# A four-layer graph network on one core: the attention query as one wide product per slot, and the layer norm of x ahead of the slot search

## What is computed

```python
h = maximum(_layernorm(x), 0);  x = x + L0(h, weight, src, dst, edge_type_16)   # sum of h[src] @ weight[type] by dst
h = maximum(_layernorm(x), 0);  x = x + L1(h, edge_index, W_l, b_l, W_r)        # mean of h[src] by dst, elu
h = maximum(_layernorm(x), 0);  x = x + L2(h, edge_index, edge_attr_32, ...)    # edge MLP, sum by dst, node MLP, layer norm
h = maximum(_layernorm(x), 0);  x = x + L3(h, edge_index, edge_type_8, rule_ids, ...)  # attention
```

## Time and profile before

| | |
|---|---|
| median of 3 runs | 2432.45 us (2432.16 to 2432.92) |
| the profiled execution | 2440.53 us, span 2438.6 us |
| busy: PE, VectorE, ScalarE, GpSimd | 1427.3, 741.7, 191.1, 1610.6 us |
| instructions | 36361 |
| first gather of layers 0 to 3 | at 77, 625, 1192 and 1806 us |

### The profile page before, as it was taken

How to read it: one execution, slowest core, us unless ns; L and a number is a source line. 1 busy time by engine, 2 the same in 40 slices (tenths; PEclk the granted TensorE clock), 3 DMA queues, 4 the chain that set the end, 5 groups by cost and what they waited for, 6 DMA issues and landing times.

```text
span 2438.6 us, 36361 instructions
## 1 busy us (share of the span) xinstructions
PE 1427.3 (59%) x7642; PEld 1254.6 (51%) x7643; DVE 741.7 (30%) x2432; ACT 191.1 (8%) x311; POOL 1610.6 (66%) x1693
## 2 busy tenths in 40 slices
PE   5586666666433333333577657666574336767686
PEld 2386666666433333333466546555443236656575
DVE  5311111111511111111532222222442234444456
ACT  3000000000000000000211111111220000000000
POOL 2577777776577777776377777777127777777530
PEclk9655555555555555555655565565655555555555
DMA  6621111111111111111233333332063323222210
GB/s 195 219 43 27 26 26 26 26 26 23 32 26 26 26 26 26 26 26 24 49 72 68 66 65 65 65 65 54 6 256 83 78 75 78 79 77 77 57 42 14
DMA packets 159011, 144.41 MB, mean 59 GB/s; under 512 B 109905, under 2 KB 111855, under 8 KB 158802
## 3 DMA queue, kind: packets, MB, share of 16 engines
q0 software_dynamic: 53888, 69.64, 13.9%
q1 hardware_dynamic: 105058, 73.94, 10.4%
HBM read 113.55 MB, written 37.28 MB: 62 GB/s over the span
## 4 chain that ended last, share of the span: by engine, by line
POOL 54%; issue 22%; PE 16%; DVE 5%; DMA 2%; ACT 1%; SPq 0%; DVEq 0%; POOLq 0%; ACTq 0%
POOL flat L467 49%; PE ps L1200 8%; POOL uvT L467 5%; PE ps L1190 5%; PE ps L1042 1%; DMA table<-flat 1%; PE ps L1016 1%; PE ps L1025 1%; DVE var L545 0%; PE ps L1055 0%; DVE uvT L538 0%; DMA flat<-table,flat 0%; DVE mean L536 0%; DVE ps L870 0%; DVE h L560 0%
## 5 line engine op out<-in xcount | busy, mean ns | idle before, releaser
L467 POOL DMA_INDIRECT flat<-table,flat x1248 | 1194.3, 957 | 491.0 <-issue 379.7
L1055 PE MATMUL ps<-flat,oh 128*128 128x64 f32 x1664 | 469.2, 431 | 490.7 <-DMA flat<-table,flat 482.4
L1055 PEld LDWEIGHTS ps<-flat,oh 128*128 128x128 f32 x1664 | 406.5, 331 | 503.9 <-issue 503.9
L627 DVE TENSOR_SCALAR oh<-iota_n,drel 128x128 f32<-128x128 f32 x1248 | 264.0, 299 | 1052.2 <-PE ps L1055 631.9
L467 POOL DMA_INDIRECT uvT<-table,idx x416 | 399.5, 960 | 230.3 <-issue 125.6
L1190 PE MATMUL ps<-qn,oh_bytes 128*128 x1248 | 164.8, 235 | 188.6 <-issue 111.0
L1190 PEld LDWEIGHTS ps<-qn,oh_bytes 128*128 128x128 bf16 x1248 | 128.7, 104 | 227.0 <-issue 198.6
L1057 PEld LDWEIGHTS ps<-ones,oh 128*128 128x128 f32 x832 | 227.3, 333 | 0.0
L1057 PE MATMUL ps<-ones,oh 128*128 128x1 f32 x832 | 221.3, 335 | 0.0
L1200 PE MATMUL ps<-flat,oh 128*128 128x65 f32 (+1 forms) x832 | 188.1, 420 | 9.9 <-DVE oh L814 5.2
L1200 PEld LDWEIGHTS ps<-flat,oh 128*128 128x128 f32 x832 | 180.6, 331 | 15.5 <-issue 13.7
(11 more groups left out here) (259 smaller groups left out, 873.6 us busy)
## 6 DMA issues: line engine op xcount, KB each, us to landing
table<-flat SPq DMA_DIRECT2D x52, 512.0 KB, 3.6
oh_bytes<-slot_node SPq DMA_DIRECT2D x104, 256.0 KB, 3.4
flat<-table,flat POOLq DMA_INDIRECT x1248
flat<-edge_attr_padded SPq DMA_DIRECT2D x416, 16.0 KB
uvT<-table,idx POOLq DMA_INDIRECT x416
edge_attr_padded<-edge_attr SPq DMA_DIRECT2D x1, 6250.0 KB
xs<-x SPq DMA_DIRECT2D x1, 768.0 KB
flat<-L_gnn_weight SPq DMA_DIRECT2D x2, 256.0 KB, 3.9
```

The source lines that it names most:

```text
L467: nc.gpsimd.indirect_dma_start(dest[:, b, j, :], None, table, at_).then_inc(gat[b], 16)
L627: last = V.tensor_scalar(oh[:, b, j, :], iota_n[:], drel[:, bass.ds(g * SG + j, 1)], None, ALU.is_equal)
L1055: last = T.matmul(acc[:, bass.ds(n[j] * D, D)], oh[:, b, j, :], rows_[:, j, :], start=False, stop=True, skip_group_check=True)
```

## The change

Two edits are made together.

**Layer 3.** The three parts of the query of one slot are no longer accumulated by three products. One product of 204 columns (`qn[:, :, n, :]`, 3 x 68) leaves them side by side in PSUM: 8 products and 8 weight loads per group. `qr_ps` has two buffers, one for each half of a group, in place of four. VectorE adds the three parts: the rule part by a reduction over 3 (48 inputs per half, in place of a copy of 16), the query by multiplying all 192 columns by the key (768 elements per half and partition, in place of 256) and summing 192 in place of 64 (1536 inputs per group, in place of 512). TensorE signals each half by itself, and starts the next group's half when VectorE has multiplied this one's. `LATE` goes: in chunk 3 the last four steps weigh two groups each, as in chunk 2, and `mix(3)` weighs none.

**Setup.** SyncE loads all of `x` ahead of `dst`. VectorE takes the first half of the layer norm, then the four instructions up to `reach`, then the second half and `rectified`, and only then the slot search. VectorE copies the first halves of blocks 0 to 5 (`EARLY`) too, right behind the slot search, and again from block 18 (`AHEAD`, was 14). The transposes of line 1006 move behind block 5, those of line 1077 from behind block 11 to behind block 15.

```diff
-        qr_ps = [ps[:, 2048 + 512 * k:2048 + 512 * k + 4 * (D + NR)] for k in range(4)]
-        room = [ps[:, 2048 + 512 * k + 4 * (D + NR):2048 + 512 * (k + 1)] for k in range(4)]
+        QP = 256
+        qr_ps = [ps[:, 2048 + 4 * QP * q:2048 + 4 * QP * (q + 1)].rearrange("p (s c) -> p s c", s=4)[:, :, 0:3 * (D + NR)]
+                 .rearrange("p s (a d) -> p s a d", a=3) for q in range(2)]
+        room = [ps[:, 2048 + 512 * k:2048 + 512 * (k + 1)] for k in range(4)]
...
-        AHEAD = 14
+        EARLY, AHEAD = 6, 18
...
-            if c == 2:
-                return [PIECES[0] + lg] if left > RING else [PIECES[0] + 8 + 2 * (lg - 8) + k for k in range(2)]
-            return [FIRST[2] + lg]
-
-        LATE = [FIRST[2] + PIECES[3] + k for k in range(PIECES[2] - PIECES[3])]
+            once = PIECES[c] - RING
+            return [FIRST[c - 1] + lg] if lg < once else [FIRST[c - 1] + once + 2 * (lg - once) + k for k in range(2)]
...
+            sp.wait_ge(s("xs_clear"), 1)
+            sp.dma_start(xs[0:NLAST, TN - 1, :], a["x"][(TN - 1) * P:N, :]).then_inc(s("x_in"), 16)
 ...
             sp.wait_ge(s("init"), INIT)
...
+            def table_half(n):
+                dve.wait_ge(s("tab_ps"), n + 1)
+                stage_free(dve, 0, n)
+                V.tensor_copy(stage[:, n % 4, 0:512], acc[:, (n % 2) * 1024:(n % 2) * 1024 + 512]).then_inc(s("tabA"), 1)
...
             dve.wait_ge(s("x_in"), 32)
-            for t0, t1 in HALVES:
-                centred(xs, t0, t1)
+            centred(xs, *HALVES[0])
+            dve.wait_ge(s("dst_in"), 32)
+            dve.wait_ge(s("const"), 9)
...
+            centred(xs, *HALVES[1])
             rectified()
...
+            for n in range(EARLY):
+                table_half(n)
+            dve.wait_ge(s("rows_ps"), 1)
+            link(V.tensor_copy(n_slots, n_ps))
...
+            dve.wait_ge(s("tabA"), AHEAD)
             for n in range(AHEAD, NT):
+                table_half(n)
...
             def before3(g, b):
-                dve.wait_ge(s("qr_ps"), g + 1)
+                dve.wait_ge(s("qr_ps"), 2 * g + 2)
                 onehots_T(1, g, b)
 
             def score(g, lg, b):
-                dve.wait_ge(s("qr_ps"), g + 3)
                 landed(dve, 3, g, b)
+                dve.wait_ge(s("scored"), g + 2)
                 for q in range(2):
-                    qr = qr_ps[2 * (b % 2) + q].rearrange("p (s d) -> p s d", s=4)
-                    V.tensor_copy(rule_e[:, bass.ds(lg * SG + 4 * q, 4), :], qr[:, :, D:D + NR])
-                    V.tensor_tensor(msg[:, b % 2, 4 * q:4 * q + 4, :], qr[:, :, 0:D], got3[:, b, 4 * q:4 * q + 4, D:2 * D], ALU.mult).then_inc(s("prod"), 1)
-                dve.wait_ge(s("prod"), 2 * (g + 1))
-                V.tensor_reduce(base[:, bass.ds(g * SG, SG)], msg[:, b % 2], AX, ALU.add).then_inc(s("scored"), 1)
+                    four = slice(4 * q, 4 * q + 4)
+                    dve.wait_ge(s("qr_ps"), 2 * g + q + 5)
+                    V.tensor_reduce(rule_e[:, bass.ds(lg * SG + 4 * q, 4), :], qr_ps[q][:, :, :, D:D + NR].rearrange("p s a r -> p s r a"), AX, ALU.add)
+                    V.tensor_tensor(msg3[:, four], qr_ps[q][:, :, :, 0:D], got3[:, b, four, D:2 * D].unsqueeze(2).broadcast_to([P, 4, 3, D]), ALU.mult).then_inc(s("prod"), 1)
+                dve.wait_ge(s("prod"), 2 * g + 4)
+                V.tensor_reduce(base[:, bass.ds(g * SG, SG)], msg3.rearrange("p s a d -> p s (a d)"), AX, ALU.add).then_inc(s("scored"), 1)
...
             for n in range(NT):
                 act.wait_ge(s("tab_ps"), n + 1)
...
-                if n < AHEAD:
+                if n == EARLY:
+                    act.wait_ge(s("tabA"), EARLY)
+                if EARLY <= n < AHEAD:
                     A.copy(stage[:, n % 4, 0:512], acc[:, at_:at_ + 512]).then_inc(s("tabA"), 1)
...
             def query(g, b, n):
-                pe.wait_ge(s("scored"), g + 1)
                 pe.wait_ge(s("ohT"), G + g + 3)
                 for q in range(2):
+                    pe.wait_ge(s("prod"), 2 * g + q + 2)
                     for j in range(4):
-                        dest = qr_ps[2 * (b % 2) + q][:, j * (D + NR):(j + 1) * (D + NR)]
-                        for part in range(3):
-                            last = T.matmul(dest, ohT[:, b % 2, 4 * q + j, :], qn[:, part, bass.ds(n[4 * q + j], 1), :].rearrange("p t d -> p (t d)"),
-                                            start=(part == 0), stop=(part == 2))
-                last.then_inc(s("qr_ps"), 1)
+                        last = T.matmul(qr_ps[q][:, j], ohT[:, b % 2, 4 * q + j, :], qn[:, :, bass.ds(n[4 * q + j], 1), :].rearrange("p a t d -> p a (t d)"), start=True, stop=True)
+                    last.then_inc(s("qr_ps"), 1)
```

More of the change, by code:

```diff
@@ L508, in _, with stage_free @@
             V.memset(dst_rows[:, SC - 1, :], 0).then_inc(s("init"), 1)
[L509 removed]
             V.memset(dprev[:, SC - 1, :], 0).then_inc(s("init"), 1)
             V.memset(dnext[:, SC - 1, :], 0).then_inc(s("init"), 1)
[L513 to L519, removed]
[L520 to L531 removed]
+            def stage_free(eng, l, n):
+                before = l * len(range(n % 4, NT, 4)) + n // 4
+                if before:
+                    eng.wait_ge(tab[n % 4], 16 * before)
+            def table_half(n):
+                dve.wait_ge(s("tab_ps"), n + 1)
+                stage_free(dve, 0, n)
+                V.tensor_copy(stage[:, n % 4, 0:512], acc[:, (n % 2) * 1024:(n % 2) * 1024 + 512]).then_inc(s("tabA"), 1)
             sums, squares = [0], [0]
@@ L562, in _ @@
             dve.wait_ge(s("x_in"), 32)
-            for t0, t1 in HALVES:
-                centred(xs, t0, t1)
-            rectified()
+            centred(xs, *HALVES[0])
+            dve.wait_ge(s("dst_in"), 32)
+            dve.wait_ge(s("const"), 9)
+            link(V.tensor_scalar(reach_i[:], dst_rows[:, :, P - 1], 7, None, ALU.arith_shift_right))
+            link(V.tensor_tensor(reach[:], reach_i[:], iota_tile[:], ALU.add))
+            link(V.tensor_scalar(slot_t[:], iota_tile[:], float(TE - 1), 1e6, ALU.is_ge, ALU.mult))
+            V.tensor_tensor(reach[:], reach[:], slot_t[:], ALU.add).then_inc(s("reach"), 1)
+            centred(xs, *HALVES[1])
+            rectified()
+            link(V.memset(pack[:, SC - 1, :, :], 0))
+            dve.sem_inc(s("pack_clear"), 1)
+            dve.wait_ge(s("reach_row"), 1)
+            for c in range(SC):
+                link(V.tensor_scalar(work[0][:, :, :].rearrange("p c k -> p (c k)"), aux[:, 1024:1024 + SC * P], iota_slot[:, c:c + 1], None, ALU.is_lt, ALU.add, accum_out=slot_t[:, c:c + 1]))
+            link(V.tensor_copy(slot_ti[:], slot_t[:]))
+            link(V.tensor_tensor(slot_n[:], iota_slot[:], slot_t[:], ALU.subtract))
+            V.tensor_scalar(slot_n128[:], slot_n[:], float(P), None, ALU.mult).then_inc(s("slot_t"), 1)
+            for n in range(EARLY):
+                table_half(n)
+            dve.wait_ge(s("rows_ps"), 1)
+            n_ps = aux[0:1, 512:512 + SLOTS].rearrange("o (g j) -> o g j", j=SG)
+            link(V.tensor_copy(n_slots, n_ps))
             link(V.tensor_copy(n_words, n_slots[:, :, 0]))
@@ L1001, in _ @@
             for c in range(SC):
-                last = T.matmul(aux[:, c * P:(c + 1) * P], reach[:, c:c + 1].broadcast_to([P, P]), ident[:], start=True, stop=True)
+                last = T.matmul(aux[:, 1024 + c * P:1024 + (c + 1) * P], reach[:, c:c + 1].broadcast_to([P, P]), ident[:], start=True, stop=True)
             last.then_inc(s("reach_row"), 1)
-            pe.wait_ge(s("slot_t"), 1)
-            for c in range(SC):
-                last = T.transpose(aux[0:1, 512 + START[c]:512 + START[c] + P], slot_n[:, c:c + 1], ident[:])
-            last.then_inc(s("rows_ps"), 1)
             def node_transposes(src, *ready):
@@ L1071, in _ @@
             pe.wait_ge(s("w0_in"), 32)
-            for n in range(AHEAD - 2):
+            for n in range(EARLY):
+                table_ps(0, n)
+            pe.wait_ge(s("slot_t"), 1)
+            for c in range(SC):
+                last = T.transpose(aux[0:1, 512 + START[c]:512 + START[c] + P], slot_n[:, c:c + 1], ident[:])
+            last.then_inc(s("rows_ps"), 1)
+            for n in range(EARLY, AHEAD - 2):
                 table_ps(0, n)
```

53 lines of the change are left out of this document (10 added, 43 removed).

## The result

The changed kernel takes 2424.55 us (median of 7 runs, 2423.04 to 2425.29) and the kernel before 2432.45 (7 runs, 2431.11 to 2433.05): ratio 0.9965, 95% interval 0.9956 to 0.9975. It is 7.9 us faster; 43.4 us were forecast, and the range of 2381 to 2408 did not hold the time. The profiled execution took 2425.13 us with a span of 2423.3.

A forecast was written before the change was run, and what follows sets the result against it. GpSimd's gathers were taken to pace layers 0 to 2 and TensorE to bind from 2132 us in layer 3; 35.4 us there plus 8.0 in the setup, 43.4 off the median 2432.45, gave 2389, range 2381 to 2408.

The forecast's parts named there:

- the third item on the query: Layer 3: TensorE waits for the previous group's half product, done 2.1 us after a query starts; nothing lost.
- the item above it: Layer 3, VectorE: a score takes about 3.9 us where it took 1.65; covered, just, by TensorE's step.
- Query of 1.4 us, step 2.0 less: Layer 3, TensorE: 8 products for 24 take 1.4 us; a step shortens by 2.0, bounds 1.0 and 2.1.
- VectorE's score 3.9 us: Layer 3: a score with three query parts takes about 3.9 us, +2.2 on 1.65.
- rival 1: Layer 3: VectorE or the array takes over, steps shorten by about 1.2; 2403 or 2407 us, chance 0.21.
- Chunk 3 even, mix(3) 8.8 us won: Layer 3's end: faster queries offset the moved sums, 0.1 us won; last mix takes 13.1 for 21.9 us.
- GpSimd's stall: Layer 3, near the end of chunk 2: GpSimd's 15.56 us wait for a score would disappear.
- Setup, 8.0 us: Before layer 0: layer norm 9.1 us earlier, first table block at 19.9 for 28.24; 8 us left.
- the margin of 1.7 us: Setup: index copies end at 52.9, VectorE's block 18 comes at 54.6; 1.7 us free for a slower fetch.
- Rival 2: Gathers: longer VectorE instructions hold GpSimd, 2 us on each of 52 groups; 2493 us, chance 0.04.
- Rival 3: Layer 3's query: columns decide, so it costs the same; 2429 us, chance 0.04.

The follow-up runs named there:

- experiments 1 and 6: 1: changed kernel with the second half's extra wait relaxed, 2389.82 us; 6: the same with query and score of the first bf16 part only, 2390.62 us.
- experiment 3: Changed kernel with the old order of chunk 2's sums, 2416.56 us; reverse, kernel before with only the new order, 2442.65 us.
- experiment 4: Changed kernel with the second half's extra wait relaxed and the old order of chunk 2's sums, 2398.04 us.

## Why the prediction was wrong

**The step that failed** is the third item on the query: "TensorE now waits for the half product of the group before; that is done 2.1 us after a query starts, while the sums take longer. Nothing is lost there." For the second half it is the product of the same group, which cannot be done before TensorE has sent it. The cost of the wait was put at nothing from a wrong reading of its number; VectorE's 0.2 + 0.95 us, both in the item above it, would have given a query of 0.86 + 1.4 + 0.86 = 3.1. The runs show 1.35 to 1.39 us of idle time in each query, a step that wins 0.4 us and not 2.0, and 34.7 us that come back when the wait is relaxed.

**Most other steps held**, as the wait relaxed shows: 2389.82 us, where 2389 was forecast. That layer 3 as a whole comes within 0.3 us of the forecast is in part luck, as misses cancel: `mix(1)` starts 0.8 us sooner than forecast and the last mix gives 9.2 us and not 8.8, but chunk 3 loses 1.4 us where 0.1 was to be won. The times below are us from the first gather of layer 3 in each trace (1806.46, 1792.15, 1790.38), for the start of each mix and of the final sums:

| | before | after | wait relaxed | forecast change | wait relaxed less before |
|---|---|---|---|---|---|
| `mix(1)` | 333.4 | 331.2 | 329.9 | -2.7 | -3.5 |
| `mix(2)` | 480.1 | 473.7 | 452.8 | -26.5 | -27.3 |
| `mix(3)` | 563.6 | 571.7 | 537.7 | -26.6 | -25.9 |
| final sums | 585.5 | 584.5 | 550.4 | -35.4 | -35.1 |

- *Query of 1.4 us, step 2.0 less*: 1.54 and 2.0 (9.85 to 7.8, 8.6 to 6.6), once the wait is relaxed. That issue sets the step was the claim; experiments 1 and 6 together show it. 16 products fewer at 2.0 us is 0.13 each, the spacing from which it was worked out. The reason given for it was incomplete: the first query of the layer, 24 products in 0.98 us, ran at the granted clock of 1.00 and the later ones at 0.50, so that its speed alone does not tell issue from clock. The query behind it does, as it starts at 1.00 too (us; busy PE, PEld, DVE, ACT, POOL; PEclk):

```profile
1826.30:1827.40 1.10, 1.04 (x25) 0.85 (x23) 0.00 (x0) 0.00 (x0) 0.80 (x2) 1.00 0.27 60
1829.50:1831.50 2.00, 1.88 (x15) 1.39 (x15) 0.22 (x1) 0.00 (x0) 1.58 (x2) 1.00 0.49 101
```

At the same clock its products stand 0.13 us apart (15 in 2.0 us), where those of the query that was issued ahead stand 0.04 apart.
- *VectorE's score 3.9 us*: 0.21 + 0.95 twice and 1.75, about 4.1. It is covered in steps of 6.6 us, so rival 1 is out.
- *Chunk 3 even, mix(3) 8.8 us won*: in after, chunk 3 loses 14.6 us (from -6.4 to +8.2 in the table) and the mix wins 9.2. The move of the sums was costed at 13.6 + 2.1 = 15.7 inside the steps and costs 18.5 (experiment 3), 2.8 more, but above all its cover, the faster query, was missing. With the fast query it pays (experiment 4), with the slow one it costs 8 us (experiment 3). This interaction is why the attention edit came out at zero.
- *GpSimd's stall*: 10.79 us are left of 15.56 in after, none when the wait is relaxed:

```profile
2288.09 0.94 POOL L470 DMA_INDIRECT uvT<-table,idx  x1 [10.79 <-DVE base L818]
```

- *Setup, 8.0 us*: 7.9 to 8.8 in the medians; at the first gather 7.86 in the two traces and 6.2 on average over all ten. `x` landed at 7.04 and not at 6.6, the first block ran at 20.13 (forecast 19.9). The index fetch handed over at 41.69, 2.2 us later than the forecast of 39.5. Of these, 0.7 are an error in the sum: from the end of the search (21.3) and the 18.9 us that the fetch takes before (14.0 to 32.94) it should have been 40.2. The index copies end at 55.14, just ahead of VectorE's copy of block 18 at 55.38, so the margin of 1.7 us was used up; the copies of the next pairs follow in their usual 2.77 us.
- *Rival 2, GpSimd held*: out, gathers are 1.25 us apart with VectorE at 68%. The Trainium skill, SBUF — State Buffer, section "Who interferes with whom", has it so for a `tensor_reduce` and for products of which one input is in PSUM, and the trace agrees.
- *Rival 3, 2429 us, "the query costs the same"*: it named the time best (2424.55), but not its cause. Its condition, that columns decide, is out by experiments 1 and 6. The rule weighed for it, in the Trainium skill, TensorE: Matmul & The Clock Gate, section "Back-to-back issue gap", gives, as an estimate, 0.17 us for 204 columns at 1.2 GHz; eight products in a row take 1.54 us, 0.19 each, so for the large product it nearly fits. The small ones stood 0.132 us apart with 68 columns, for which an estimate by the rule gives 0.06. The section itself gives the rule for a product by itself and says that it comes out too low for small products, as it leaves out the weight load; the prediction left that out.

The range was too narrow because every rival priced the engines, and none allowed for a wait that does not mean what its author read.

## What to carry to other kernels

Work out a changed semaphore wait with numbers for each pass of its loop (here `g` = 1, `q` = 1: which signal is number 3?), and see whether it needs something that the waiting instruction itself makes possible; an edit that replaces one wait for a group by one for each half can make producer and consumer take turns. Two edits in one change may carry each other: moving work into a loop is free or even a gain only while something else sets the loop's pace, so look at it with and without the other edit. And when a step is bound by issue, the number of instructions is its price; here the query's columns could be cut to a third and VectorE's score to less than half, and the step did not move.

## What was not expected of the hardware

- On one chip the same kernel took 3009 us and not 2432, at nearly the same granted clock (0.531 to 0.536 against 0.546 to 0.551 in the profiled executions) and with gathers still 1.25 us apart where they ran. TensorE stood idle for 11 to 19 us at a time (27 to 28 at the longest), with "issue" as the only reason shown; in chunk 2 of layer 3 it did so in every second step:

```profile
2708.86 1.54 PE L1205 MATMUL ps<-qn,oh_bytes 128*128 x8 [16.52 <-issue]
...
2716.65 1.54 PE L1205 MATMUL ps<-qn,oh_bytes 128*128 x8 [2.68 <-issue]
...
2737.88 1.54 PE L1205 MATMUL ps<-qn,oh_bytes 128*128 x8 [16.14 <-issue]
```

What held them back no row shows, and it stays open. Only the steps between such stalls can be read there, and they agree with the usual chip (1.54, 7.8, 10.9 us).
- The four gaps of the last mix are not free: four sums in them cost 9.2 us with the old query and 10.6 to 10.9 with the new one, 2.3 to 2.7 each, against 4.1 in a step that TensorE's issue sets and 1.4 (5.5 / 4) in the four steps that GpSimd comes to set.
- A query queued behind 5.9 us of other products ran its 24 products in 0.98 us. The query behind it, at the same granted clock of 1.00 for its first 2 us, stood at 0.13 us a product and took 3.33: a product costs a third when the work ahead of it is long enough for the issue to run on.

The version to keep is the changed kernel with the wait relaxed, 2389.82 us: 42.8 us (1.8%) under the kernel before, and the best of all that ran.
